# Products of shifted keys in three VectorE instructions a turn instead of eight

## What is computed

```
xn  = layernorm(x)
gnn = segment_sum(edge_weight * xn[dst], src)                  # 100000 edges
q, k, v = per head (8 heads of 32) of xn @ Wqkv.T + bqkv
qn, kn  = q, k scaled to length, times scale (and temperature)
kv_mod[i,j,e] = sum over nodes of kn[i] * kn[j] * v1[e]         # all products of two key features
kv[d,e]       = sum over nodes of kn[d] * v1[e]
y = 0.5 * (qn qn kv_mod) + scale^2 * (qn kv) + scale^4 * sum(v1); divide by its first column
x = x + gnn + y @ Wproj.T + bproj
x = x + layernorm(layernorm(x) + top-2-of-16 mixture of experts (256 -> 512 -> 256)) 
```

## Time and profile before

| what | value |
|---|---|
| median of 3 runs | 2320.89 us |
| profiled execution, from the first to the last instruction | 2504.8 us |
| its granted TensorE clock | 0.875 |
| busy: TensorE, VectorE, ScalarE, GpSimd | 77%, 61%, 44%, 55% |
| L1418, the products of shifted keys | 392 instructions, 248.1 us busy |
| L795, the gathers | 832 instructions, 854.4 us busy |

### The profile page before, as it was taken

How to read it: one execution, slowest core, us unless ns; L and a number is a source line. 1 busy time by engine, 2 the same in 40 slices (tenths; PEclk the granted TensorE clock), 3 DMA queues, 4 the chain that set the end, 5 groups by cost and what they waited for, 6 DMA issues and landing times.

```text
span 2504.8 us, 43129 instructions
## 1 busy us (share of the span) xinstructions
PE 1933.7 (77%) x11937; PEld 1281.9 (51%) x11938; DVE 1523.4 (61%) x3822; ACT 1094.8 (44%) x3069; POOL 1365.7 (55%) x1265
## 2 busy tenths in 40 slices
PE   5656765788889888788888888887553999999940
PEld 3434542455555554444444434445453888888830
DVE  6988888888888888444444444555343333333348
ACT  4635552333333333445554455444441444444433
POOL 1263444776677766666666666663553455433333
PEclk8768888899999999899999999997555999999975
DMA  8300001222232222233333333346453455555574
GB/s 298 127 29 23 28 28 27 87 88 86 87 90 87 89 88 86 85 97 95 93 95 93 95 99 95 92 93 123 158 184 104 91 95 95 95 95 95 94 201 154
DMA packets 160920, 248.21 MB, mean 99 GB/s; under 512 B 26161, under 2 KB 122803, under 8 KB 160756
## 3 DMA queue, kind: packets, MB, share of 16 engines
q0 software_dynamic: 64496, 144.32, 23.4%
q1 hardware_dynamic: 93300, 99.37, 13.0%
q10 hardware_dynamic: 2960, 2.57, 0.3%
HBM read 182.25 MB, written 63.91 MB: 98 GB/s over the span
## 4 chain that ended last, share of the span: by engine, by line
PE 35%; issue 7%; another core or an unknown queue 7%; ACT 5%; DVE 5%; DMA 1%; ACTq 1%; DVEq 0%; SPq 0%; POOL 0%; POOLq 0%
PE bqk L2121 9%; PE bank L2101 8%; PE b L1852 4%; PE bank L1977 3%; PE bqk L1988 2%; PE b L1866 2%; ACT big L934 2%; ACT big L993 1%; PE bank L2061 1%; PE b L2091 1%; ACT mid L993 1%; PE b L1854 1%; DVE big L1634 1%; DVE st L1160 1%
## 5 line engine op out<-in xcount | busy, mean ns | idle before, releaser
L795 POOL DMA_INDIRECT big<-xn_dram,big x832 | 854.4, 1027 | 426.3 <-issue 220.6
L1852 PE MATMUL b<-big 128*128 128x256 f32 x1468 | 420.7, 414 | 25.2 <-issue 14.9
L1852 PEld LDWEIGHTS b<-big 128*128 128x128 f32 x1468 | 276.1, 203 | 202.6 <-issue 107.4
L1400 DVE TENSOR_TENSOR acc<-acc,b 128x256 f32 x465 | 193.3, 416 | 302.2 <-PE b L1852 152.8
L824 POOL DMA_INDIRECT sum_dram<-mid,idxy x113 | 175.4, 1552 | 279.1 <-ACT mid L1067 218.8
L934 ACT ACTIVATE big<-big 128x128 f32<-128x128 f32 x832 | 265.3, 401 | 41.4 <-DVE big L1376 17.8
L2121 PE MATMUL bqk<-big,mid 128*128 x896 | 223.8, 393 | 25.8 <-issue 24.4
L2101 PEld LDWEIGHTS bank<-late,mid 128*128 128x128 f32 x1808 | 223.3, 195 | 5.9
L2101 PE MATMUL bank<-late,mid 128*128 128x128 f32 x1808 | 223.5, 278 | 0.0
L993 ACT ACTIVATE big<-bank 128x512 f32<-128x512 f32 (+1 forms) x208 | 104.8, 576 | 235.8 <-remote 82.7
L2121 PEld LDWEIGHTS bqk<-big,mid 128*128 128x128 f32 x896 | 162.1, 191 | 65.5 <-issue 46.6
(11 more groups left out here) (336 smaller groups left out, 3493.3 us busy)
## 6 DMA issues: line engine op xcount, KB each, us to landing
big<-w SPq DMA_DIRECT2D x32, 512.0 KB
mid<-z_dram SPq DMA_DIRECT2D x114, 130.0 KB, 2.1
mid<-b SPq DMA_DIRECT2D x113, 128.0 KB
big<-xn_dram,big POOLq DMA_INDIRECT x832
sum_dram<-mid SPq DMA_DIRECT2D x19, 640.0 KB, 13.6
big<-sum_dram SPq DMA_DIRECT2D x18, 640.0 KB, 8.9
acc<-x_pad SPq DMA_DIRECT2D x10, 640.0 KB, 6.8
xn_dram<-big SPq DMA_DIRECT2D x9, 640.0 KB, 3.2
```

Source lines behind the costliest of these rows:

```text
L795: pool.indirect_dma_start(out=gx[t % GB], out_offset=None, in_=xn_dram, in_offset=bass.IndirectOffsetOnAxis(ap=dstA[:, t:t + 1], axis=0)). ...
L1400: v.tensor_tensor(mine, mine, ps_pair[p % 2][:, C * j:C * (j + 1)], ALU.add).then_inc(s_add, 1)
L1852: a = pe.matmul(ps_pair[p % 2][:, 0:C], wd[t % (2 * EB)], gx[t % GB], start=(j == 0), stop=(j == 1))
```

## The change

`shifted` takes a first head h and a number n of heads, and its three access patterns get one more dimension, n steps of 48 columns in `kd` and of 512 in `kk`. A turn calls it with 3, 3 and 2 heads where it called it 3, 3 and 2 times with one. Elements, places between the edges and semaphores stay.

```diff
-            def shifted(k, h):
-
-                return v.tensor_tensor(kk[k][:, h], window(kd[k], h * DW, [[0, 16], [1, D]]),
-                                       window(kd[k], h * DW + 1, [[1, 16], [1, D]]), ALU.mult)
+            def shifted(k, h, n):
+
+                return v.tensor_tensor(kk[k][:, h:h + n], window(kd[k], h * DW, [[DW, n], [0, 16], [1, D]]),
+                                       window(kd[k], h * DW + 1, [[DW, n], [1, 16], [1, D]]), ALU.mult)
...
-                for h in range(3):
-                    shifted(k, h)
+                shifted(k, 0, 3)
                 edges(1, 2)
-                for h in range(3, 6):
-                    shifted(k, h)
+                shifted(k, 3, 3)
                 edges(2, 3)
-                shifted(k, 6)
-                shifted(k, 7).then_inc(s_kk, 1)
+                shifted(k, 6, 2).then_inc(s_kk, 1)
                 edges(3, KE)
```

## The result

The changed kernel takes 2338.36 us (median of 4 runs, 2335.87 to 2339.87). The kernel before took 2320.68 us on the same chip (4 runs, 2318.12 to 2321.14). The ratio is 1.0078, interval 1.0065 to 1.0091: 17.7 us slower. The forecast was 2339.0, 18 us slower.

A forecast was written before the change was run, and what follows sets the result against it. VectorE's own chain bounds the key-stage turn now; after merging, GpSimd's 8 gathers, held by longer locks, would. 45 turns x (12.4 - 12.0) = +18 us on 2320.9 gives 2339 us, range 2304 to 2364.

The forecast's parts named there:

- VectorE term: Key stage, VectorE: three merged products cost 4.47 us a turn instead of 4.80, 0.33 us less; extra dimension free.
- lock: Key stage: a GpSimd DMA starting beside a VectorE instruction with two SBUF inputs waits for its end, then runs 0.83 us.
- first rival: Key stage: GpSimd still fits with locks up to 1.6 us a turn, VectorE's gain arrives; 2306 us, chance 0.28.
- four signs: Profile after: gather mean 1.25 to 1.3 us, GpSimd's TensorE wait near 0, L1400 idle above 42.9 at edges two to four.
- turn of 12.4: Key stage: forecast length in us of a turn with edges, the middle of 11.67 and 13.1, against 12.0 before.
- the walk: One changed key-stage turn followed with both engines' phases: 7 gathers fit in 11.49 us where 8 are needed.
- second reckoning: Key stage: 10.06 us of undisturbed gathers plus 2.4 to 2.7 us of lock waits gives turns of 12.5 to 12.8.
- the sum: Whole kernel: 45 turns with edges x (12.4 - 12.0) gives +18 us.
- four turns without edges: Start of key stage: they give nothing, since VectorE's 1.98 us wait after them takes up their 1.3 us.
- Carrying over the difference: Whole kernel: the +18 us from the 2504.8 us profile is added unscaled to the runs' median of 2320.9.

The follow-up runs named there:

- e8: Kernel before with each 512-element product replaced by a one-input reduce that copies 512 elements, all gathers made: 2315.08 us, ratio 0.9967.
- e9: Changed kernel with one-input reduces of 1536, 1536 and 1024 elements in place of its products: 2301.46 us, ratio 0.9913.
- e5: Changed kernel with every second gather left out, TensorE using the other gather's rows: 2280.93 us, ratio 0.9833, turn 11.55 us.
- e3: Changed kernel with both three-head groups split, 1 then 2 heads (1,2 / 1,2 / 2): 2340.57 us, ratio 1.0093 to before.
- e2: Changed kernel with both three-head groups split, 2 then 1 heads (2,1 / 2,1 / 2): 2310.58 us, ratio 0.9959 to before.
- second profile: Kernel before, unchanged, profiled again because its first profile ran 183.9 us over the median: one run of 2315.59 us, span 2313.8.
- e1: Changed kernel with only the second three-head group split, 2 then 1 heads (3 / 2,1 / 2): 2304.66 us, ratio 0.9933 to before.

## Why the prediction was right

**The VectorE term was exact.** Products of 1536 and 1024 elements last 1748 and 1216 ns (forecast 1.75 and 1.21), and the additional dimension costs nothing. The first two intervals, without edges and gathers, went from 9.48 to 9.14 and 9.13 us: 0.34, forecast 0.33.

**The lock was what the prediction said.** In the changed kernel, from 460 to 940 us, 115 gathers that start under a product are held, and each ends 0.82 to 0.84 us after that product; the next starts 0.30 later. The long ones last mostly 1.7 to 1.9 us (near 2 forecast). The section "SBUF: two separate sides" of the page SBUF — State Buffer of the Trainium skill describes this rule, and e8 with e9 (17.7 us lost with two inputs, 13.6 gained with one) agrees with it. The advice to merge, read alone, gave the first rival's 2306.

**GpSimd became the bound, by the four signs named.** L795's mean is 1252 ns (1.25 to 1.3 forecast). Its wait for TensorE is 7.9 us in 26 waits, no more than the usual gap (near 0 forecast). L1400's idle time rose to 66.5 us, and in the turn shown it lies at edges 2 and 3. A turn is 12.32 us (12.4 forecast). Halving the gathers (e5) gives the whole VectorE gain and more.

**The size was right partly by luck.** The turn of 12.4 was the middle between 11.67 and 13.1, and taken as a steady turn. The kernel has no such turn. VectorE's own pace does run, for two turns, one of 11.49 us in which 8 gathers start and one of 11.58 with the walk's 7, as long as buffers are in hand. Then comes one of 14.07 with 9, in which VectorE waits about 2.3 us and GpSimd catches up: (11.49 + 11.58 + 14.07) / 3 = 12.38. This triple stands there seven times; the other turns lie between 11.5 and 16.9. The forecast's second reckoning fits better than the middle: 8 gathers at 1.257 and 2.4 to 2.7 us of locks gave 12.5 to 12.8, and the locks cost 2.4. I did not follow the walk past its first round, where it would have shown the debt build up and be paid in one turn. The weak point shows in e3: the same mean turn of 12.32 us comes there from another pattern (turns of 11.62 to 15.8), so a mean between two bounds says little, when the order of two pieces alone moves the kernel by the 30 us between e2 and e3. Two smaller things went unseen and partly balance: the sum left out the intervals ahead of the edges (below) and the debt of 8 gathers that is paid in the query stage, about 5 us.

**One statement was wrong.** The four turns without edges were to give nothing, for a wait of 1.98 us behind them. The first three intervals gave 0.34, 0.35 and 0.46, and the one that holds the wait fell from 24.09 to 23.29 us: 1.9 us together. What VectorE waited for there came earlier as well. The sum of 45 turns x 0.4 left this out; with it, 16.1 us would stand for the key stage, where 14.3 were measured.

**The odd profile did no harm.** Carrying over the difference and not the ratio was right: of the excess of 191 us over the second profile only 8.9 are in the key stage (a turn of 12.10 against 11.95; the forecast took 12.0).

**The first rival** was not far: it needed locks of up to 1.6 us a turn. In the changed kernel they cost 8 x (1.252 - 0.953) = 2.4; in e1 they cost 8 x (1.144 - 0.953) = 1.5, its turn is 11.66 as the rival had it, and its time of 2304.66 is the rival's 2306.

## What to carry to other kernels

Before merging two-input VectorE instructions, look at whether GpSimd issues DMAs beside them and how much idle time it has in a turn: each such instruction, if both inputs are in SBUF, holds a gather at least until its end, so merging lengthens the locks while it shortens VectorE. Merge only as far as the other engine still fits. Of the cuts tried here, those with four products a turn were best (2304.7 and 2305.3 us against 2320.7 with eight and 2338.4 with three), and the order of long and short pieces counts as much as their number. A walk through one turn with both engines' phases finds this; follow it until it closes on itself with every resource level, the buffers too.

## What was not expected of the hardware

- The order of two back-to-back instructions, 1024 and 512 elements, is worth 30.0 us over the kernel (2310.58 against 2340.57), because GpSimd gets in between two pieces only if it asked during the first.
- It does not always get in there: in the kernel before with half the gathers 23 were held over the end of one two-input instruction and through one or more behind it, up to 3.1 us in all, although none of these instructions lasts over 0.70. The cause is open.
- A two-input instruction behind a fill holds a gather from the time of the fill on: a gather of 2.99 us where 0.95 is undisturbed. Behind a one-input instruction of 1.74 us it does not.
- A fill's record begins late: at 703.74 after L1400 that began at 703.12, where a product begins 0.33 after L1400's start. Fills of 512, 1024 and 1536 elements show 485, 912 and 1338 ns.
